# A Mamba layer and an FFN on one core: y and the next exponents between the two halves of the gate's projection

## The reference, cut to what matters

```python
x = x + attn(_layernorm(x), ...)      # x: 4 x 256 x 512, fp32
x = x + ffn(_layernorm(x), ...)
...
proj = jnp.einsum('bsd,ed->bse', x, in_proj_w)
gate = proj[..., :INTER]
hBC = proj[..., INTER:INTER + CONV_DIM]
...
hBC = jax.nn.silu(conv(hBC))          # causal, 4 taps
hs, Bm, Cm = split(hBC)
...
L = jnp.exp(_segsum(A_dt))
Y_diag = jnp.einsum('bzlhn,bzshn,bhzls,bzshp->bzlhp', Cc, Bc, L, xch)
...
Y = (Y_diag + Y_off).reshape(b, s, H, P) + hs * D[None, None, :, None]
g = y * jax.nn.silu(gate)
...
return jnp.einsum('bsi,oi->bso', out, out_proj_w)
```

## Time and profile before

| | us |
|---|---|
| median of 3 runs | 1724.89 |
| lowest and highest | 1723.56, 1725.48 |
| profiled execution, its time | 1725.6 |
| profiled execution, its span | 1723.5 |

### The profile page before, as it was taken

The page is one execution under the profiler, slowest core; times in us unless marked ns, Lnnn a source line. Parts: engine busy times, 40 slices in busy tenths (PEclk is TensorE's granted clock), DMA queues, the critical chain, the costliest instruction groups (busy, mean ns, idle before and its releaser), DMA issues.

```text
span 1723.5 us, 38952 instructions
## 1 busy us (share of the span) xinstructions
PE 1696.8 (98%) x12596; PEld 1393.7 (81%) x12596; DVE 1252.2 (73%) x1882; ACT 851.1 (49%) x1301; POOL 1203.7 (70%) x874
## 2 busy tenths in 40 slices
PE   6999999999999999999999999999999999999998
PEld 5788888888888888888888888888888887788887
DVE  7888549863887288728883788468846887777777
ACT  4766346634664366536652665356634662422221
POOL 4699659964997489757985799469955987533330
PEclk9999999999999999999999999999999999999999
DMA  3333013301221123202320232023302212111101
GB/s 103 102 92 93 13 52 91 93 25 50 80 87 43 31 85 89 55 22 88 85 65 19 74 92 75 19 62 93 87 6 61 89 56 64 50 37 49 49 13 49
DMA packets 71342, 107.23 MB, mean 62 GB/s; under 512 B 16741, under 2 KB 25061, under 8 KB 71305
## 3 DMA queue, kind: packets, MB, share of 16 engines
q1 hardware_dynamic: 70296, 105.38, 20.8%
q10 hardware_dynamic: 1008, 1.38, 0.2%
HBM read 103.51 MB, written 3.15 MB: 62 GB/s over the span
## 4 chain that ended last, share of the span: by engine, by line
PE 95%; DVE 2%; POOL 1%; ACT 1%; issue 1%; DMA 1%; SPq 0%; ACTq 0%; POOLq 0%
PE proj L921 18%; PE proj L923 17%; PE proj L922 17%; PE y L1089 9%; PE y L1062 7%; PE y L1064 6%; PE y L1063 6%; PE y L1076 3%; PE y L921 2%; PE y L923 1%; PE y L922 1%; PE decay L1036 1%; PE decay L921 1%; PE decay L923 1%; PE decay L922 1%
## 5 line engine op out<-in xcount | busy, mean ns | idle before, releaser
L921 PE MATMUL proj<-xhi,w_hi 128*128 128x512 f32 x1072 | 431.4, 402 | 0.3 <-DVE gate L1300 0.3
L923 PE MATMUL proj<-xhi,w_lo 128*128 128x512 f32 x1072 | 419.5, 391 | 0.0
L922 PE MATMUL proj<-xlo,w_hi 128*128 128x512 f32 x1072 | 418.3, 390 | 0.0
L521 POOL TENSOR_TENSOR g_lo<-gated,g_hi 128x512 fp32r<-128x512 f32 x127 | 162.5, 1282 | 186.6 <-ACT g_hi L792 186.6
L1279 DVE SCALAR_TENSOR_TENSOR v<-proj,par_sb,v 128x510 f32<-128x510 f32 x378 | 275.2, 742 | 20.8 <-DVE v L1279 9.7
L921 PEld LDWEIGHTS proj<-xhi,w_hi 128*128 128x128 f32 x1072 | 201.5, 188 | 54.3 <-issue 14.3
L923 PEld LDWEIGHTS proj<-xhi,w_lo 128*128 128x128 f32 x1072 | 201.5, 188 | 43.8
L922 PEld LDWEIGHTS proj<-xlo,w_hi 128*128 128x128 f32 x1072 | 201.9, 188 | 37.8
L478 POOL TENSOR_TENSOR w_lo<-w_raw,w_hi 128x512 fp32r<-128x512 f32 x144 | 182.6, 1289 | 56.7 <-ACT w_hi L662 56.7
L539 POOL TENSOR_TENSOR gated<-hs,gate 128x512 f32 (+1 forms) x126 | 188.7, 1520 | 45.8 <-DVE hs L1414 45.8
L681 ACT ACTIVATE v<-proj,par_sb 128x512 f32<-128x512 f32 x126 | 98.2, 779 | 236.3 <-PE proj L923 236.3
(11 more groups left out here) (204 smaller groups left out, 3276.2 us busy)
## 6 DMA issues: line engine op xcount, KB each, us to landing
w_raw<-in_win SPq DMA_DIRECT2D x144, 256.0 KB, 2.7
fade_l<-faded SPq DMA_DIRECT2D x128, 256.0 KB, 3.3
wo_raw<-in_wout SPq DMA_DIRECT2D x64, 256.0 KB, 2.7
M<-in_w SPq DMA_DIRECT2D x14, 512.0 KB, 3.8
row_r<-rows SPq DMA_DIRECT2D x256, 3.0 KB
row_l<-rows SPq DMA_DIRECT2D x256, 3.0 KB
cb<-in_w SPq DMA_DIRECT2D x7, 512.0 KB, 3.3
out<-resid SPq DMA_DIRECT2D x8, 256.0 KB, 2.0
```

The lines of the kernel that those rows point to most:

```text
L521: e.tensor_tensor(g_lo[:, i % 2, :, :], tokens(t, kk), g_hi[:, i % 2, :, :].bitcast(F32), ALU.subtract)\
L921: e.matmul(o, hi_l, hi_r, start=first, stop=False)
L922: e.matmul(o, hi_l, lo_r, start=False, stop=False)
L923: return e.matmul(o, lo_l, hi_r, start=False, stop=last)
```

## The change

In PE's step, `unit(2)` moves ahead of `y()` and of the exponents. They then stand between `unit(2)` and `unit(3)`, the gate's halves. Nothing is added or removed, and the other engines' programs are the same.

```diff
@@ -1122,11 +1122,12 @@
                     unit(1)
                 else:
                     out_block(g, 0, False)
+                if nxt:
+                    unit(2)
                 y()
                 if ahead:
                     exponents(g, j + 1, 1 - par_)
                 if nxt:
-                    unit(2)
                     unit(3)
```

## The result

The changed kernel takes **1959.72 us** (median of 4 runs, 1957.35 to 1959.84) against 1724.54: the ratio is 1.1362, with a 95% interval of 1.1348 to 1.1375. That is 235 us more, slower as forecast and inside the range, 37 us above the forecast of 1923.

The account below looks back on a forecast made before the run. The prediction took PE, busy 98% of the span, as the bound. The profiled 1725.6 us plus 197 us for two new waits of PE and their restarts gave 1923 us, with a range of 1880 to 1990.

Parts of the forecast that it names:

- PE's list: PE's work in a step, 14.92 us between transposes, sets the step; its sum doesn't change, so almost nothing can be gained.
- The first wait: Ahead of unit(2): PE waits 2.01 us for DVE's filter of half 0 to free proj[0], in each of 63 steps.
- The second wait: Ahead of the next unit(0): PE waits 1.0 us for `gate_silu` of half 0 to free proj[0].
- U: The start of unit(2) in a step, forecast 5.62 us after the transposes start.
- both arms: Ahead of `gate_silu` 0: ACT's list ends at U+8.92 and DVE's additions and `hs_silu` at about U+8.9.
- What follows next: At unit(1): `gate_silu` of half 1 ends near U+12.9, needed at U+13.3, so it costs nothing.
- The sum: Over the run: 55 steps of 18.1 against 14.92 us (176), 7 last tiles (19), one tile (2.5), together 197 us.
- One sign that the prediction named: In the changed kernel's profile: PE's busy time stays as before.
- Rival 1: TensorE's clock falls behind pauses, 1.6 us each: 1974 us if every second step, 2024 if every step; chance 0.30.
- Rival 2: Only the wait at unit(2) comes, since `gate_silu` 0 is ready with unit(3)'s end: 1858 us; chance 0.09.
- Rival 3: unit(2) finds proj[0] free, so the kernel isn't slower: 1725 us within a few us; chance 0.03.
- The bound by `hs_silu`: On DVE, `hs_silu` varies from 681 to 1614 ns: no gain when short, +11 us over 55 steps when long.

Follow-up runs that it names:

- the filter first: Changed kernel, with DVE running the filter of half 0 ahead of `times_dt`: 1841.65 us, ratio 1.0686.
- the exponents alone: Kernel before, with only the exponents moved to between unit(2) and unit(3), y staying ahead of both: 1801.86 us, ratio 1.0455.
- y alone: Changed kernel, with the exponents put back ahead of unit(2), so that only y stands behind unit(2): 1915.70 us, ratio 1.1115.
- the runs with extra matmuls: Changed kernel, with unused 128x512 matmuls on PE between unit(1) and unit(2): six gave 1924.96 us, one gave 1923.97 us.
- the gate first: Changed kernel, ACT doing `hs_tanh` 1 and `gate_tanh` 0 ahead of both `bounded`, DVE `gate_silu` 0 ahead of the additions to y: 1866.05 us, ratio 1.0827.
- the kernel with y waiting: Kernel before, with DVE filtering half 0 ahead of `times_dt`, so that y waits for xfade: 1890.89 us, ratio 1.0971.

## Why the prediction was right, point by point

- **PE's list is the bound and doesn't shrink.** Right: after the exponents the next unit follows in 0.32 as before, and no piece in the steps shown here is shorter than before.
- **The first wait.** Right in cause and size: unit(2) started 5.50 (odd tiles) and 5.68 (even tiles) behind the transposes, where 5.62 was taken for all. With the second wait removed it stood alone, and with the filter first it shrank by 82 us on record.
- **The second wait.** Right. From U = 505.88 the exponents came at U+5.57 (5.49 in the forecast), `bounded` at U+6.00 (5.92), the end of `gate_tanh` at U+8.97 (8.92), `gate_silu` at U+9.00 (8.95), unit(0) at U+9.74 (9.7). That both arms, ACT's and DVE's, come out nearly equal was right as well: the run with the exponents alone frees DVE's arm and the wait stays, the run with y alone frees ACT's arm and it stays too, and the run that takes the gate ahead on both engines removes it.
- **What follows next.** Right: `gate_silu` of half 1 ended at U+12.87 (12.9) and nothing waited for it.
- **The sum.** 197 was forecast for the two waits and their restarts, 201 measured by the runs with extra matmuls. The step was 18.12 in the forecast's own pieces; in the trace it is 18.14 where the clock didn't fall, and 18.18 over all 55 in the two runs with extra matmuls. The 7 last tiles of groups cost 2.6 each and the tile before the very last 1.8, forecast with 2.7 and 2.5. One sign that the prediction named didn't come: PE's busy time isn't as before. It grew by 72, and half of that has nothing to do with the clock.
- **Rival 1, the clock.** Here is nearly the whole miss. The forecast gave this rival 0.30 and put its own term for the clock at nothing; there were 22 falls more than before, 34.8 us, 1.58 each (1.6 in the rival's price). The sum of forecast and this term is 1958. By the prediction's own sign, a granted clock clearly below 0.99, this part of the forecast was wrong: the mean was 0.979. The true case lies between the forecast and the rival's fall in every second step, nearer to the rival, and the time stayed inside the range because the range had been drawn to hold that rival. What misled was one row, the wait of 2.17 behind which the clock had stayed; the even tiles' pause is shorter than that and the clock fell in 22 of 31. The stretch at 1480 in the earlier trace rows lies ahead of the matmul at 1482.24; the one behind it in the kernel before says the same:

```profile
1482.00:1484.00 2.00, 1.75 (x9) 1.48 (x10) 1.90 (x5) 0.04 (x1) 2.00 (x1) 1.00 0.10 41
```

So the row was read rightly, but one case in which the clock stayed was no ground to expect it in 63. The Trainium skill (TensorE: Matmul & The Clock Gate, A second HAM failure mode: psum-queue depth-cycling) spoke for this rival, and the trace agrees with it here: 22 of 55 inner steps have a fall. The Trainium skill (TensorE: Matmul & The Clock Gate, Why this matters for your kernels) warns only of pauses between bursts that are longer than any inside these groups. These are 2.1 at most and the clock fell all the same, so the measurement decides against reading that advice as an all-clear.
- **Rival 2, only the first wait.** Fell: the second wait is on record 62 times. **Rival 3, not slower**, fell with the first row of waits.
- **The bound by `hs_silu`.** In the changed kernel it lasted 1.14 in the step shown and hid behind `gate_tanh`, so its spread cost nothing there, as said for the short end. In the run with y alone, where nothing hides it, it showed. What the prediction took as the reason for the spread, POOL at work beside it, fits the trace of the kernel before: its 10 executions with POOL idle beside them lasted 0.68 each, the 117 with POOL at work throughout 0.68 to 1.62, 1.29 on average.

**What stays open** is what decides whether the clock falls. It isn't the length of the pause alone: the same pauses (113.9 on record) gave 22 falls in inner steps of the changed kernel and 4 with the gate first; longer pauses (2.3 on record) in the kernel with y waiting gave 11, fewer than the changed kernel's with 1.8 on record; the exponents in the pause left 11 falls, one full matmul in the pause left none. I didn't try to settle it further.

## What to carry to other kernels

When PE is the bound and always busy, look at what each piece of its list is waiting room for. A piece that moves takes its cover away from the waits behind its old place, and it delays everything on the other engines that is queued behind its result, in their program order; both can be priced from one step of the timelines before anything is run. Price the pauses of PE twice, once as time and once as a risk for its clock.

## What the runs showed of the hardware that was not expected

In this program a pause of PE of some 2.05 us was enough to bring the granted clock to its lower level behind it, in 22 of the 31 even inner tiles. One matmul of 128x512 placed in the pause took all of these falls away, while four bf16 matmuls with a contraction of 15 rows, in the run with y alone, left 11. The falls were worth 1.8% of the run. Why they came in some steps and not in others with the same pause is open.
